# Folding the key-value sums into the output weights, and scaling the queries before their transposes

## The reference

```
x = x + attn_a(layernorm(x))                  # 16 heads of 16 features
q, k = feature_map(h @ Wq + bq), feature_map(h @ Wk + bk);  v = h @ Wv + bv
kv = einsum('bkhd,bkhm->bhdm', k, v)          # per batch and head, 16x16
out = einsum('bqhd,bhdm->bqhm', q, kv)
normalizer = maximum(einsum('bqhd,bkhd->bqh', q, k), 1e-6)
x = x + (out / normalizer) @ Wo + bo
x = x + ffn(layernorm(x))                     # squared relu, 256 -> 128 -> 256
x = x + attn_b(layernorm(x))                  # acts on 16 tokens of a batch only
x = x + ffn(layernorm(x))
```

## Time and profile before

| | us |
|---|---|
| Median of 3 runs | 432.75 |
| Lowest and highest run | 432.47, 434.18 |
| Profiled execution, span from the first to the last instruction | 432.7 |
| TensorE (PE) busy | 416.6 |
| VectorE (DVE) busy | 316.3 |
| ScalarE (ACT) busy | 217.6 |
| GpSimd (POOL) busy | 217.1 |

### The profile page before, as it was taken

How to read it: one execution, slowest core, us unless ns; L and a number is a source line. 1 busy time by engine, 2 the same in 40 slices (tenths; PEclk the granted TensorE clock), 3 DMA queues, 4 the chain that set the end, 5 groups by cost and what they waited for, 6 DMA issues and landing times.

```text
span 432.7 us, 7753 instructions
## 1 busy us (share of the span) xinstructions
PE 416.6 (96%) x2570; PEld 345.7 (80%) x2570; DVE 316.3 (73%) x707; ACT 217.6 (50%) x383; POOL 217.1 (50%) x317
## 2 busy tenths in 40 slices
PE   8998999999999999899999999999999999999993
PEld 5787889988987988889788886787887787787862
DVE  6769977676668766647878887877778767787864
ACT  3766777778777775326434342343244324334341
POOL 3675776776677764031345336534516416514532
PEclk9999999999999999999999999999999999999998
DMA  8701221111100000300110111011001010011103
GB/s 264 245 7 46 57 88 54 51 49 48 48 0 0 2 2 1 101 0 6 51 52 20 36 51 52 2 51 50 21 31 35 18 52 27 26 51 50 50 4 106
DMA packets 22793, 20.59 MB, mean 48 GB/s; under 512 B 3271, under 2 KB 22733, under 8 KB 22733
## 3 DMA queue, kind: packets, MB, share of 16 engines
q1 hardware_dynamic: 22172, 19.32, 14.1%
q10 hardware_dynamic: 560, 0.52, 0.4%
HBM read 11.32 MB, written 8.45 MB: 46 GB/s over the span
## 4 chain that ended last, share of the span: by engine, by line
PE 68%; DVE 8%; ACT 7%; POOL 7%; issue 5%; SPq 2%; DMA 1%; DVEq 1%; POOLq 0%; ACTq 0%
PE PB L1462 7%; PE PT L1504 6%; PE PA L1462 6%; PE PB L1483 6%; PE PA L1538 4%; PE PA L1544 4%; PE PA L1539 3%; PE PT L1548 3%; PE PA L1473 3%; ACT scratch L568 3%; PE PB L1510 3%; POOL ln_rstd L441 2%; PE PG L1334 2%; POOL ln_rstd L439 2%; DVE ln_bn L800 2%
## 5 line engine op out<-in xcount | busy, mean ns | idle before, releaser
L491 POOL TENSOR_TENSOR ln_a<-ln_bn 128x4 f32<-128x4 f32 x32 | 6.5, 203 | 136.1 <-DVE ln_bn L1003 136.1
L463 POOL TENSOR_TENSOR xn_pair<-scratch,xn_pair 128x1024 fp32r<-128x1024 f32 x16 | 38.4, 2402 | 18.9 <-ACT xn_pair L579 18.9
L883 DVE SCALAR_TENSOR_TENSOR scratch<-scratch,PB 128x512 f32<-128x512 f32 x32 | 20.9, 684 | 36.4 <-ACT scratch L615 36.3
L1003 DVE BATCH_NORM_STATS2 ln_bn<-x_all 128x6 f32<-128x256 f32 x128 | 44.9, 412 | 0.9
L568 ACT ACTIVATE scratch<-x_all,ln_shift,ln_rstd 128x255 f32 (+1 forms) x60 | 31.2, 593 | 22.6 <-POOL ln_shift L445 22.6
L452 POOL TENSOR_TENSOR x_all<-x_all,wvo 128x1024 f32 (+1 forms) x16 | 38.6, 2410 | 0.1
L452 POOL TENSOR_TENSOR x_all<-x_all,ob_rows 128x1024 f32<-128x1024 f32 x16 | 37.7, 2356 | 0.0
L1307 PE MATMUL PB<-wk_hi,xt_hi 128*128 128x256 f32 x128 | 36.9, 288 | 0.6 <-DVE xt_lo L828 0.4
L1309 PE MATMUL PB<-wk_hi,xt_lo 128*128 128x256 f32 x128 | 36.2, 283 | 0.0
L1308 PE MATMUL PB<-wk_lo,xt_hi 128*128 128x256 f32 x128 | 36.2, 283 | 0.0
L736 ACT ACTIVATE scratch<-PA,ln_rsq 128x256 f32<-128x256 f32 x30 | 12.6, 471 | 45.4 <-PE PA L1462 40.2
(11 more groups left out here) (247 smaller groups left out, 1139.0 us busy)
## 6 DMA issues: line engine op xcount, KB each, us to landing
x_all<-n_L_attn_a_inputs_q_dram SPq DMA_DIRECT2D x15, 512.0 KB, 3.5
out_dram<-x_all SPq DMA_DIRECT2D x15, 512.0 KB, 3.1
out_dram<-x_all SPq DMA_DIRECT2D x2, 256.0 KB, 2.2
x_all<-n_L_attn_a_inputs_q_dram ACTq DMA_DIRECT2D x2, 128.0 KB, 3.0
x_all<-n_L_attn_a_inputs_q_dram SPq DMA_DIRECT2D x2, 128.0 KB, 2.7
setup<-in_L_attn_a_Wk_dram SPq DMA_DIRECT2D x1, 256.0 KB, 4.6
setup<-in_L_attn_a_Wq_dram ACTq DMA_DIRECT2D x1, 256.0 KB, 5.0
wvo<-in_L_attn_a_Wv_dram SPq DMA_DIRECT2D x1, 256.0 KB, 6.7
```

What stands on the lines that cost most here:

```text
L463: nc.gpsimd.tensor_tensor(xn_pair[:, :, 1, :], xn[g % 2], xn_pair[:, :, 0, :].bitcast(F32), ALU.subtract).then_inc(x_lo, 1)
L1003: nc.vector.bn_stats(ln_bn[:, slot, t:t + 1, :], x_tile(n, t)).then_inc(bn, 1)
```

## The change

In the first pass the key and the query weights stand side by side, and a tile's keys and queries come from one product with 512 columns (kq_product); the queries now have tokens on the partitions too. Exponentials and feature maps go by pairs of tiles or by single tiles, and VectorE takes the low part of the keys in two halves (k_low). ScalarE makes the high part of x before it normalises the next group. The sums over a batch come out already turned, as 24 products of 256 columns, so their transposes go. At the end of a batch the masked key-value product is multiplied by the output weights, and the result is split into m_hi and m_lo (m_product, m_high, m_low), which stand in for wo_hi and wo_lo; the key sums are spread over all partitions (ksum). GpSimd's last two bias adds of the first pass come after its last x_low and the first key_products.

In the second pass the product L1483 goes. GpSimd multiplies a group's queries by the key sums (key_products), VectorE sums the products by head, clamps them, takes the reciprocal and scales the queries in place (inverse_norms); this is done one step ahead, for group i + 1 in step i. TensorE turns the scaled queries, right after the transposes of x. The add of PB goes in two halves. The core of the diff, by engine: GpSimd, then VectorE, then TensorE.

```diff
-        q_all = sb("q_all", [P, NG * C, GT])
-        kv_all = sb("kv_all", [P, B * C, KVW])
+        q_all = sb("q_all", [P, NG * T, D])
+        m_hi, m_lo = sb("m_hi", [P, (B - 1) * C, D], F32R), sb("m_lo", [P, (B - 1) * C, D], F32R)
...
+            def key_products(i):
+
+                n = group_of(i)
+                pool.wait_ge(kq_done, KQ_DONE * (n + 1))
+                pool.wait_ge(ksum_done, i % B + 1)
+                ge(pool, n_step, 2 * i - 1)
+                nc.gpsimd.tensor_tensor(qk.rearrange("p (t d) -> p t d", d=D), x_like(q_all, n),
+                                        ksum[:, i % B:i % B + 1, :].to_broadcast([P, T, D]), ALU.mult).then_inc(n_prod, 1)
...
             x_low(NG - 1, NG - 1)
+            key_products(0)
+            add_bo(NG - 2)
             add_bo(NG - 1)
...
+                if runs(i + 1):
+                    key_products(i + 1)
                 if runs(v):
                     four_variances(1, v, bn3, var3)
-                if runs(r):
-                    pool.wait_ge(t2_mm, C * (r + 1))
-                    add_row(nr, ob_rows, ob_added)
                 chain(i, 1)
                 if runs(v) and v < NG - 1:
                     pool.wait_ge(f4_scaled, 2 * (v + 1))
                     last = x_all[:, nv * T + 2:(nv + 1) * T, :]
                     nc.gpsimd.tensor_tensor(last, last, y3, ALU.add).then_inc(out_pool, 1)
+                if runs(r):
+                    pool.wait_ge(t2_mm, C * (r + 1))
+                    add_row(nr, ob_rows, ob_added)
                 chain(i, 2)
                 if runs(r):
...
+            def k_low(n, h):
+                half = slice(2 * h, 2 * h + 2)
+                dve.wait_ge(hi_done, 3 * n + 2 + h)
+                nc.vector.tensor_tensor(k_lo[:, half, :], k_tok[:, half, :], k_hi[:, half, :].bitcast(F32), ALU.subtract).then_inc(k_lo_done, 1)
...
+            def inverse_norms(i):
+
+                dve.wait_ge(n_prod, i + 1)
+                nc.vector.reduce_sum(norm_sb[:, :], qk.rearrange("p (k e) -> p k e", e=HD), AX).then_inc(n_step, 1)
+                dve.wait_ge(n_step, 2 * i + 1)
+                nc.vector.tensor_scalar(norm_sb[:, :], norm_sb[:, :], NORM_EPS, None, ALU.max).then_inc(n_step, 1)
+                dve.wait_ge(n_step, 2 * i + 2)
+                nc.vector.reciprocal(norm_inv[:, :], norm_sb[:, :]).then_inc(n_inv, 1)
+                dve.wait_ge(n_inv, i + 1)
+                n = group_of(i)
+                heads_q = q_all[:, n * T:(n + 1) * T, :].rearrange("p t (h e) -> p (t h) e", e=HD)
+                nc.vector.tensor_tensor(heads_q, heads_q, norm_inv[:, :].unsqueeze(2).to_broadcast([P, T * H, HD]),
+                                        ALU.mult).then_inc(q_scaled, 1)
+
...
+                    features(n, slice(0, 2), 0, EXP_Q01)
+                    features(n, slice(0, 2), 1, EXP_Q01)
+                    if later_batch:
+                        mask_kv(b - 1)
+                    features(n, slice(2, 3), 0, EXP_Q2)
+                    features(n, slice(3, 4), 0, EXP_K3)
+                    k_low(n, 0)
+                    k_low(n, 1)
...
-                    for k0, nb, reg in regions:
-                        nc.vector.tensor_tensor(o_tok[:, k0:k0 + nb, :].rearrange("p k (h e) -> p k h e", e=HD),
-                                                reg.rearrange("p (k w) -> p k w", w=KVW)[:, :, 0:P].rearrange("p k (h e) -> p k h e", e=HD),
-                                                norm_inv[:, k0:k0 + nb, :].unsqueeze(3).to_broadcast([P, nb, HC, HD]),
-                                                ALU.mult).then_inc(o_done, 1)
...
                 chain(i, 1)
-                if runs(i):
-
-                    for c in range(C):
-                        dve.wait_ge(o_hi_done, C * i + c + 1)
-                        ge(dve, w_mm, i)
-                        nc.vector.tensor_tensor(o_lo[:, c, :], PB[:, c, :], o_hi[:, c, :].bitcast(F32),
-                                                ALU.subtract).then_inc(o_lo_done, 1)
+                if runs(i + 1):
+                    inverse_norms(i + 1)
...
-                    nc.vector.tensor_tensor(x_group(nr), four(PB), x_group(nr), ALU.add).then_inc(f2_added, 1)
+                    for h in range(2):
+                        two = x_all[:, nr * T + 2 * h:nr * T + 2 * h + 2, :]
+                        dve.wait_ge(f2_mm, 2 * r + h + 1)
+                        nc.vector.tensor_tensor(two, four(PB)[:, 2 * h:2 * h + 2, :], two, ALU.add).then_inc(f2_added, 1)
...
+            def kq_product(t, cols, done):
+
+                dst = kq_bank(t)[:, cols]
+                for c in range(C):
+                    hi, lo = (x[:, c, t * P:(t + 1) * P] for x in (xt_hi, xt_lo))
+                    mm(dst, hi, w_hi[:, c, cols], start=(c == 0), stop=False)
+                    mm(dst, hi, w_lo[:, c, cols], start=False, stop=False)
+                    last = mm(dst, lo, w_hi[:, c, cols], start=False, stop=(c == C - 1))
...
+                for c in range(C):
+                    last = mm(PG[:, 1, c * D:(c + 1) * D], kv_t[:, c * P:(c + 1) * P], wo_raw[:, c, :], start=True, stop=True)
+                last.then_inc(m_mm, 1)
...
-                    for k in (6, 7, 0, 1, 2, 3, 4, 5):
-                        t, c = k // C, k % C
-                        if k == 0:
-                            ge(pe, f2_added, i - 1)
-                        dst = PB[:, k // 3, (k % 3) * KVW:(k % 3 + 1) * KVW] if k < 6 else PT[:, 1, (k - 6) * KVW:(k - 5) * KVW]
-                        last = mm(dst, q_all[:, (b * G + g) * C + c, t * P:(t + 1) * P], kv_all[:, b * C + c, :], start=True, stop=True)
-                    last.then_inc(o_mm, 1)
...
+                    pe.wait_ge(q_scaled, i + 1)
+                    for c in range(C):
+                        if runs(v):
+                            pe.wait_ge(f2_added, 2 * v + c + 1)
+                        for t in range(T):
+                            last = nc.tensor.transpose(PB[:, c, t * P:(t + 1) * P], q_all[:, (b * G + g) * T + t, c * P:(c + 1) * P], ident[:, :])
+                        last.then_inc(qt_mm, 1)
...
-                                mm(four(PA)[:, t, :], hi, wo_hi[:, c, :], start=(c == 0), stop=False)
-                                mm(four(PA)[:, t, :], hi, wo_lo[:, c, :], start=False, stop=False)
+                                mm(four(PA)[:, t, :], hi, m_h[:, c, :], start=(c == 0), stop=False)
+                                mm(four(PA)[:, t, :], hi, m_l[:, c, :], start=False, stop=False)
```

More of the change, by code:

```diff
@@ L24 @@
 NE = 8
-KVW = P + HC
 LN_EPS = 1e-5
@@ L474, in _ @@
                 x_low(n - 1, n - 1)
-            with pool.Fori(1, B) as b:
+            with pool.Fori(1, B - 1) as b:
                 for g in range(G):
@@ L480, in _ @@
                     x_low(n - 1, g + 1)
+            for n in range((B - 1) * G, NG):
+                ln1(n)
+                if n < NG - 1:
+                    add_bo(n - 1)
+                x_low(n - 1, n - 1)
             x_low(NG - 1, NG - 1)
+            key_products(0)
+            add_bo(NG - 2)
             add_bo(NG - 1)
@@ L607, in pass1 @@
                     first = isinstance(n, int) and n == 0
+                    later_batch = g == 0 and not (isinstance(b, int) and b == 0)
+                    x_high(n, g)
                     if not first and not (last and g == G - 1):
                         ln1(n + 1, g + 1)
[L610 to L616 removed]
+                    ge_apart(act, "act", k_lo_done, 2 * n)
@@ L617, in pass1 @@
+                    act.wait_ge(kq_mm, T * n + 2)
+                    exponential(n, slice(0, 2), 0)
+                    exponential(n, slice(0, 2), 1)
                     if first:
                         ln1(1, 1)
-                    if g == 0 and not (isinstance(b, int) and b == 0):
-                        transposed_g(b - 1)
-                    for h in range(2):
-                        act.wait_ge(k_done, 2 * n + h + 1)
-                        nc.scalar.activation(k_hi[:, 2 * h:2 * h + 2, :], k_tok[:, 2 * h:2 * h + 2, :], ACT.Copy).then_inc(hi_done, 1)
@@ L1458, in fold_ffn_product, with down @@
                 last.then_inc(fold_mm, 1)
-            def down(pair, h, done):
+            def down(pair, h, done, halves=False):
                 for t in range(T):
                     last = mm(four(pair)[:, t, :], h[:, t * P:(t + 1) * P], ws2[:, :], start=True, stop=True)
-                last.then_inc(done, 1)
+                    if t == T - 1 or halves and t % 2:
+                        last.then_inc(done, 1)
             def step(g, b):
@@ L1543, in step @@
                             for t in tiles:
-                                last = mm(four(PA)[:, t, :], o_lo[:, c, t * P:(t + 1) * P], wo_hi[:, c, :], start=False, stop=(c == C - 1))
+                                last = mm(four(PA)[:, t, :], o_lo[:, c, t * P:(t + 1) * P], m_h[:, c, :], start=False, stop=(c == C - 1))
                     last.then_inc(w_mm, 1)
@@ L1550, in step @@
```

(2 more changed lines are left out.)

367 lines of the change are left out of this document (183 added, 184 removed).

## The result

| | before | after |
|---|---|---|
| Median | 432.61 us (4 runs) | 475.42 us (4 runs, 474.74 to 475.74) |
| Ratio, 95% interval | | 1.098 (1.095 to 1.101) |
| Span of the profiled execution | 432.7 | 473.0 |

The kernel became slower, by 42.8 us where 16.7 were worked out; 475 lies above the range. The profiled execution after took 474.74 us in all, 1.7 more than its span; the front part took the span for the whole time, which a difference of two spans does not notice.

A forecast was written before the change was run, and what follows sets the result against it. TensorE was taken as the bound in both passes, the loop of VectorE and GpSimd as the next. Terms of 2.8 + 7 - 1.5 - 2 + 3.5 + 1.9 + 5 = +16.7 on 432.7 gave 449.4, forecast 450 us, range 421 to 463.

The forecast's parts named there:

- the plain step: Second pass, a step without small attention work: 14.5 us forecast, against 13.45 for one before the change.
- step 1: Second pass, a step that is all TensorE: gains most of the removed 2.10, -1.5 us, bounds -2.1 and 0.
- step 15: Second pass, no next group to prepare, so neither new product nor scaling: -2 us, bounds -2.1 and 0.
- the tail: End of the kernel: GpSimd's last full add now stands behind the half add, +1.9 us, bounds 0 and +2.4.
- Steps 5 to 14: Second pass, steps with small attention work: +0.7 us a step, +7 in all; bounds per step -1.3 and +1.05.
- rival three: Second pass: GpSimd's full add gets the port before the clamp as well, 0.65 us more a step, 458; chance 0.13.
- the clamp goes first: Plain step of the second pass: the clamp waits 0.15 us for GpSimd's half add, then runs ahead of its full add.
- Rival four: TensorE's clock falls in the new gaps: 5.7 us a step, over 500 in all; chance 0.03.
- First pass "+0.2 in ten plain groups": VectorE's split subtraction stands still up to 1.2 us at GpSimd's add: +0.2 a group, within +5 for the pass.
- step 0 "+3.5": Start of the second pass: first queries scaled in a row of 3.15 us, two GpSimd adds delaying it: +3.5, bounds 0 and +6.

The follow-up runs named there:

- the first experiment: GpSimd's full bias add of the second pass waits until VectorE has scaled the queries, against the changed kernel; 450.43 us, 1.039 to the kernel before.

## Why the prediction was wrong

The direction, the mechanism and the plain step held: the bound moved from TensorE to the loop of VectorE and GpSimd, the scaling stood 1.5 (forecast 1.75) behind the full add in plain steps, L1088 idled 1.2 to 1.5 there, and step 1, step 15 and the tail came within 0.5. The rule of the Trainium skill ("SBUF — State Buffer", Who interferes with whom) that a reduction never takes part held too: 16 head sums took 1.15 to 1.22 us, whatever GpSimd did.

Three steps failed.

*Steps 5 to 14, "+0.7, nearer to the plain step".* They cost 1.7 each on average, but not evenly: steps 5, 7, 10, 12 and 13 cost 2.4 to 5.1 each, and the others came out 0.3 to 0.9 shorter than before. The upper bound had been the plain step, on the argument that work in the first slot shortens the wait. In the five long steps the small attention's work lengthened the wait instead: the clamp stood behind two or three instructions (3.99 in step 5, 2.61 in step 7), the scaling behind two (3.20 in step 10, 3.19 in step 12), and in step 13 a multiply of the small attention stood behind the full add. These are also the steps of this stretch in which the clock fell. The clamp's part is rival three's mechanism, priced there at 0.65 for a clamp behind one add: the full add started before the clamp in seven steps (1, 2, 5, 7, 8, 9 and 11). The order "the clamp goes first" was read from one place, where the waiting instruction was a subtraction of two tiles. Such instructions were let in ahead of a waiting add in steps 0, 10 and 12 too; the clamp was not in steps 5 and 7. What decides was not found. The 25 us of the first experiment hold these meetings together with the clock behind them.

*Rival four, given 0.03.* The clock did fall, in seven places. The argument against it was the stretch of 4.20 us at the end of the program with full clock. The row was true and ended too early. TensorE had no work left behind it, and the same trace has the fall 0.4 us further on, with TensorE still idle:

```profile
430.40:432.69 2.29, 0.00 (x0) 0.00 (x0) 0.00 (x0) 0.00 (x0) 0.00 (x0) 0.50 0.62 206
```

So the trace of before already showed the clock falling in idle time, and the stretch could not bear the conclusion. The rival's price, half of each step in every step, was far too high: filling gaps gave 10 us back in five steps. The Trainium skill ("TensorE: Matmul & The Clock Gate", Why this matters for your kernels) warns of idle gaps between bursts of work. The trace agrees with it in kind: the falls came within or just behind gaps of 2.25 to 4.53 us. The length of a gap did not tell them apart: 2.25 in step 4 had a fall, 2.36 in step 3 and 2.40 in step 2 had none.

*First pass "+0.2 in ten plain groups" and step 0 "+3.5".* Both meetings were named and undersized. The halves of a group stood up to 2.2 us, not 1.2; 12 to 13 us of the loss went when two GpSimd instructions were exchanged. In step 0 VectorE's halves took 5.28 behind two adds (182.33 to 187.47), and the scaling behind the next product 2.74. By the trace of the experiment that moved the adds, they make 3.7 of the 8.0, a shorter fall of the clock among them. What the other 4.3 are was not separated.

So, of 42.8 us: 25 go with the meeting in the second pass (the falls of the clock behind it among them), 12 to 13 with the order in the first pass, and some 5 are left, which the product a step earlier, with the two adds in step 0, took away. Only when the new meetings were taken apart too was the kernel without the product faster than the kernel before, by 3.5 to 6 us.

## What to carry to other kernels

Before a VectorE instruction on two SBUF tiles, or a clamp from SBUF to SBUF, is put on the path, list what GpSimd may run at that time, the whole queue behind its first instruction, and count its sum as the longest possible wait. Before a row is used against a rival, look at what stands just behind the row. When the bound leaves TensorE, price each gap twice: once as idle time, and once as the work behind it at the lower clock. A wait that keeps the shorter program waiting can be the cheaper order, but it moves all that is queued behind it.

## What the runs showed of the hardware

- A clamp of 128x64, 0.20 us alone, took 3.99 behind three GpSimd instructions in a row, a memset among them; it was not let in between. A scaling of 128x1024, 1.22 alone, took 3.20 behind two and was let in ahead of a third, which then took 3.33 where 2.38 is usual.
- The granted clock fell within or behind some gaps and not others of the same size: a gap of 2.36 in step 3 had no fall, one of 2.25 in step 4 had one, and step 7 had one in one of two kernels with the same instructions there. In step 7 of the first experiment it fell behind two gaps of 0.90 and 1.03. What decides was not found.
- More work on TensorE made a kernel 10 us faster, by keeping its clock at 2.4 GHz in five steps.
